# Edge tiles of 124 rows instead of 128 in a three-layer relational graph kernel with gathers from HBM

## The reference

```python
def rgcn_layer(h, W, root, bias):            # W: [8, 256, 256]
    agg = segment_sum(h[src], edge_type * 6250 + dst, 8 * 6250).reshape(8, 6250, 256)
    return einsum('rnd,rde->ne', agg, W) + h @ root + bias
xn = layernorm(x)
h = relu(rgcn_layer(xn, W0, root0, bias0))
h = relu(rgcn_layer(h, W1, root1, bias1))
h = sigmoid(rgcn_layer(h, W2, root2, bias2))
x = x + h + mix(xn)                          # linear attention, 8 heads; MLP 256 -> 1024 -> 256
out = x + moe(layernorm(x))                  # 8 experts, top 2
```

## Time and profile before

| quantity | value |
|---|---|
| time, median of 3 runs | 8040.71 us (8016.86 to 8065.2) |
| profiled execution, span from the first to the last instruction | 6522.0 us |
| profiled execution, its own total time | not given; the span is what the profile tells |
| TensorE matmul, busy | 5410.7 us (83%) |
| TensorE weight load, busy | 4060.0 us (62%) |
| GpSimd, busy | 4625.3 us (71%) |
| VectorE, busy | 2019.4 us (31%) |
| ScalarE, busy | 1061.6 us (16%) |
| moved by DMA | 887.88 MB, mean 136 GB/s |

### The profile page before, as it was taken

The page is one execution under the profiler, slowest core; times in us unless marked ns, Lnnn a source line. Parts: engine busy times, 40 slices in busy tenths (PEclk is TensorE's granted clock), DMA queues, the critical chain, the costliest instruction groups (busy, mean ns, idle before and its releaser), DMA issues.

```text
span 6522.0 us, 82564 instructions
## 1 busy us (share of the span) xinstructions
PE 5410.7 (83%) x22990; PEld 4060.0 (62%) x22990; DVE 2019.4 (31%) x5385; ACT 1061.6 (16%) x2756; POOL 4625.3 (71%) x4909
## 2 busy tenths in 40 slices
PE   8977777777777778888888888887888888888888
PEld 4445555555555546666666666666777777777776
DVE  3321211122222223332333333333444444444444
ACT  2211111111111111111111111111222222222222
POOL 1057777777777767777777777776777777777776
PEclk9989898889898889999999999999999999999999
DMA  6654444444444444544554444444433333433333
GB/s 195 180 155 137 137 137 137 137 137 137 137 137 137 137 143 144 147 146 146 147 148 146 146 145 146 147 146 149 116 115 115 115 115 115 115 115 115 116 115 93
DMA packets 354380, 887.88 MB, mean 136 GB/s; under 512 B 86234, under 2 KB 179294, under 8 KB 335623
## 3 DMA queue, kind: packets, MB, share of 16 engines
q0 software_dynamic: 232080, 633.91, 33.0%
q10 hardware_dynamic: 114178, 243.16, 12.8%
q1 hardware_dynamic: 7740, 5.99, 0.3%
HBM read 697.11 MB, written 185.60 MB: 135 GB/s over the span
## 4 chain that ended last, share of the span: by engine, by line
POOL 44%; PE 30%; issue 15%; ACTq 5%; DMA 3%; ACT 1%; POOLq 1%; DVE 0%; DVEq 0%; SPq 0%
POOL ring L501 44%; PE ps_out L1403 11%; PE ps_y L1371 8%; PE ps_tr L1570 2%; PE ps_b L1558 2%; DMA ring<-table,gather_idx 2%; PE ps_c L1371 1%; PE ps_b L1371 1%; PE ps_c L1558 1%; ACTq L619 1%; ACTq L740 1%; ACTq L699 1%; ACT y_stage L517 1%; PE ps_y L1656 1%; ACTq L527 1%
## 5 line engine op out<-in xcount | busy, mean ns | idle before, releaser
L501 POOL DMA_INDIRECT ring<-table,gather_idx x4836 | 4580.7, 947 | 1519.4 <-issue 1487.8
L1403 PE MATMUL ps_out<-ring,onehot 128*125 x8400 | 2238.3, 419 | 709.7 <-SPq L428 671.1
L1403 PEld LDWEIGHTS ps_out<-ring,onehot 128*125 128x125 f32 x8400 | 1699.0, 209 | 1131.0 <-issue 857.7
L1371 PE MATMUL ps_y<-W,hT 128*125 128x512 f32 (+1 forms) x2400 | 1016.9, 564 | 0.9 <-ACT hT L564 0.9
L835 DVE COPY y_stage<-ps_y 125x512 f32<-125x512 f32 x150 | 103.7, 692 | 2425.6 <-PE ps_y L1371 2393.6
L1403 PE MATMUL ps_out<-ring,onehot_more 128*125 x2448 | 661.3, 421 | 131.9 <-SPq L428 87.4
L1371 PEld LDWEIGHTS ps_y<-W,hT 128*125 128x125 f32 x2400 | 455.8, 192 | 400.1 <-issue 372.7
L994 DVE TENSOR_TENSOR onehot<-targets,ps_out 128x500 f32<-128x500 f32 x1050 | 646.4, 671 | 172.1 <-issue 117.1
L1403 PEld LDWEIGHTS ps_out<-ring,onehot_more 128*125 128x125 f32 x2448 | 479.5, 205 | 286.8 <-issue 214.7
L517 ACT COPY y_stage<-ps_y 125x512 f32<-125x512 f32 x350 | 204.6, 585 | 1659.1 <-PE ps_y L1371 1653.8
L994 DVE TENSOR_TENSOR onehot_more<-targets,ps_out 128x250 f32<-128x250 f32 x612 | 240.9, 414 | 608.4 <-PE ps_out L1403 490.2
(11 more groups left out here) (193 smaller groups left out, 3208.2 us busy)
## 6 DMA issues: line engine op xcount, KB each, us to landing
table<-y_stage ACTq DMA_DIRECT2D x147, 896.0 KB
ring<-table,gather_idx POOLq DMA_INDIRECT x4836, 2.9
table<-y_stage ACTq DMA_DIRECT2D x147, 104.0 KB
xn_in<-xn_scratch ACTq DMA_DIRECT2D x100, 125.0 KB
base<-y_stage ACTq DMA_DIRECT2D x100, 125.0 KB
base_in<-base ACTq DMA_DIRECT2D x100, 125.0 KB
x_in<-in_x_dram ACTq DMA_DIRECT2D x75, 125.0 KB
xn_scratch<-xn_in ACTq DMA_DIRECT2D x50, 125.0 KB
```

Of the source, the lines that this page charges most:

```text
L501: nc.gpsimd.indirect_dma_start(ring[0:n, c * D:(c + 1) * D], None, table[l], bass.IndirectOffsetOnAxis(ap=gather_idx[0:n, tile:tile + 1].b ...
L1371: last = nc.tensor.matmul(BANK[phase][b][0:WIN, 0:n], hT[parity][:, k, :], W[:, k, b * 2 * D:b * 2 * D + n], start=(k == 0), stop=(k == K ...
L1403: return nc.tensor.matmul(ps_out[w % 2][0:WIN, 0:D], lhsT, ring[:, bass.ds(slot + j * D, D)], start=first, stop=last)
```

## The change

TILE becomes 124. A gather moves 124 rows into the first 124 partitions of `ring`, the one-hot matrices have 124 partitions, and the multiplies have 124 rows to add over. The edge lists are loaded with 124 edges to a tile: blocks of 128 tiles remain, with rows of 124 numbers (496 bytes) instead of 128 (512 bytes). RING, TILES and STATIC stay as they are.

206,250 edges now make 1664 tiles (the last with 38 edges) in 416 chunks, all filled, so 4992 gathers in the three layers. Both before and after there are 13 blocks of 128 tiles. In the last, partly filled block there were 75 whole tiles and are 127. From the drawn edge list the units a layer, borders counted twice, come to 465 after, against 452 before.

```diff
--- before.py
+++ after.py
@@ -26,7 +26,7 @@
 
 WIN = 125
 WIN_A = 112
-TILE = 128
+TILE = 124
 TILES = 4
 RING = 8
 STATIC = 7
@@ -92,8 +92,8 @@
         gather_idx = sb("gather_idx", [128, TB * 128], I32)
         targets = sb("targets", [128, TB * 128])
         ring = sb("ring", [128, RING * TILES * D])
-        onehot = [sb(f"onehot{i}", [128, TILES, WIN]) for i in range(STATIC)]
-        onehot_more = [sb(f"onehot_more{i}", [128, HALF, WIN]) for i in range(2)]
+        onehot = [sb(f"onehot{i}", [TILE, TILES, WIN]) for i in range(STATIC)]
+        onehot_more = [sb(f"onehot_more{i}", [TILE, HALF, WIN]) for i in range(2)]
         W = sb("W", [128, K, ROWS * D])
         bias_bc = sb("bias_bc", [WIN, 3, D])
         y_stage = [sb(f"y_stage{i}", [WIN, ROWS * D]) for i in range(2)]
@@ -176,7 +176,7 @@
         bounds_row = qk_all[0:1, :, :].rearrange("p a b -> p (a b)")[:, 0:7 * NB_INTS].rearrange("p (i n) -> p i n", i=7)
 
 
-        PREP = TB * 128
+        PREP = TB * TILE
         prep_i = big[:, 0:PREP].bitcast(I32)
         prep_f = big[:, PREP:2 * PREP]
         prep_d = big[:, 2 * PREP:3 * PREP].bitcast(I32)
@@ -370,7 +370,7 @@
             sp.wait_ge(prep_zeroed, 1)
             for name, dst in (("src", prep_i), ("edge_type_8", prep_t), ("dst", prep_d)):
                 a = t[name]
-                v = dst[:, 0:TB * 128].rearrange("p (b f) -> p b f", f=128)
+                v = dst[:, 0:TB * TILE].rearrange("p (b f) -> p b f", f=TILE)
                 if full_blocks:
                     sp.dma_start(v[:, 0:full_blocks, :], a[0:full_blocks * 128 * TILE]
                                  .rearrange("(b p f) -> p b f", p=128, f=TILE)).then_inc(edges_loaded, 16)
@@ -436,12 +436,12 @@
         @block.gpsimd
         def _(pool):
 
-            lo = full_blocks * 128
-            nc.gpsimd.memset(prep_i[:, lo:TB * 128], 0)
-            nc.gpsimd.memset(prep_t[:, lo:TB * 128], 0)
+            lo = full_blocks * TILE
+            nc.gpsimd.memset(prep_i[:, lo:TB * TILE], 0)
+            nc.gpsimd.memset(prep_t[:, lo:TB * TILE], 0)
 
             nc.gpsimd.memset(order_b[:, ordC - 1:ordC], PADDED)
-            nc.gpsimd.memset(prep_d[:, lo:TB * 128], PADDED).then_inc(prep_zeroed, 1)
+            nc.gpsimd.memset(prep_d[:, lo:TB * TILE], PADDED).then_inc(prep_zeroed, 1)
             nc.gpsimd.memset(ident[:], 1.0).then_inc(consts_made, 1)
             pool.wait_ge(consts_made, 1)
             nc.gpsimd.affine_select(out=ident[:], in_=ident[:], compare_op=ALU.is_equal, fill=0.0,
@@ -496,8 +496,9 @@
                         for j in range(TILES):
                             c = s * TILES + j
                             tile = chunk * TILES + j
-                            n = min(TILE, edges - tile * TILE)
-                            assert n > 0
+                            left = edges - tile * TILE
+                            n = min(TILE, left) if left > 0 else TILE
+                            assert n > 1
                             nc.gpsimd.indirect_dma_start(
                                 ring[0:n, c * D:(c + 1) * D], None, table[l],
                                 bass.IndirectOffsetOnAxis(ap=gather_idx[0:n, tile:tile + 1].bitcast(U32), axis=0)
@@ -881,8 +882,8 @@
 
                 for i in (2 * b, 2 * b + 1):
                     dve.wait_ge(prep_tr, i + 1)
-                    nc.vector.tensor_copy((gather_idx, targets)[i % 2][:, b * 128:(b + 1) * 128],
-                                          ps_out[i % 2][:, 0:128]).then_inc(prep_ev, 1)
+                    nc.vector.tensor_copy((gather_idx, targets)[i % 2][0:TILE, b * 128:(b + 1) * 128],
+                                          ps_out[i % 2][0:TILE, 0:128]).then_inc(prep_ev, 1)
 
             def units_before():
 
@@ -992,8 +993,8 @@
 
             def onehots(out, n, nodes, col, count):
                 return nc.vector.tensor_tensor(
-                    out, targets[:, bass.ds(col, count)].unsqueeze(2).broadcast_to([128, count, n]),
-                    nodes.unsqueeze(1).broadcast_to([128, count, n]), ALU.is_equal)
+                    out, targets[0:TILE, bass.ds(col, count)].unsqueeze(2).broadcast_to([TILE, count, n]),
+                    nodes[0:TILE, :].unsqueeze(1).broadcast_to([TILE, count, n]), ALU.is_equal)
 
             def set_nodes(w):
 
@@ -1310,7 +1311,7 @@
                 else:
                     pe.wait_ge(prep_ev, 2 * b)
                 for src, half in ((prep_f, 0), (prep_df, 1)):
-                    nc.tensor.transpose(ps_out[half][:, 0:128], src[:, b * 128:(b + 1) * 128],
+                    nc.tensor.transpose(ps_out[half][0:TILE, 0:128], src[:, b * TILE:(b + 1) * TILE],
                                         ident[:, :]).then_inc(prep_tr, 1)
 
             def vectors_transposed():
@@ -1401,7 +1402,7 @@
 
             def add_tile(w, lhsT, slot, j, first=False, last=False):
                 return nc.tensor.matmul(ps_out[w % 2][0:WIN, 0:D], lhsT,
-                                        ring[:, bass.ds(slot + j * D, D)], start=first, stop=last)
+                                        ring[0:TILE, bass.ds(slot + j * D, D)], start=first, stop=last)
 
             def unit(l, w, i):
```

## The result

The changed kernel takes 8462.96 us (median of 4 runs, 8461.52 to 8464.06), the kernel before 8035.37 us (4 runs, 8016.86 to 8065.2). The ratio is 1.053, 95% interval 1.0506 to 1.0553: 427.6 us slower, where 215 us were forecast. The sign was right and the size was not; 8463 us lies above the range.

What follows compares the result with a forecast made beforehand. GpSimd's gather beat was taken as the bound. 156 more gathers added 184 us (8225) or 234 us (8275), all other terms 0; the middle, 8250 us (+2.6%), was forecast, range 8170 to 8340 us.

Steps and rivals of the forecast that it cites:

- the data of the gathers: Indirect queue's transfers: row numbers 16 does not divide still go over all 16 engines, far from the limit; cost 0.
- the gathers: GpSimd's gather line, main term: 156 more gathers at a beat of 1.248 us, +184 us.
- over 4 engines: Rival, gather transfers: 4 us more if the four engines change; 10,881 us if always the same four, chance 0.03.
- The sum's basis: Whole run: +184 us if 1518.7 us outside the span stand apart, +234 if gathers carry them; middle 8250 us.
- upper end: Whole run: 1518.7 us spread over the gathers, beat 1.564 us, 156 more gathers less 10 us for rows: 8275 us.
- what bounds the kernel now: GpSimd's gather line: engine full at a steady 1.25 us beat, gathers 6056 of 6522 us.
- Count of gathers: GpSimd's gather line: 4836 gathers become 4992, adding 184 to 234 us.
- Edge lists: Phase 0 loads: 0 to 27 us more, covered by 30.7 us before VectorE needs them; taken as 0.
- TensorE and VectorE at 0: Multiplies and one-hot work: 39 more units, 22.5 us a layer on TensorE, hidden under waits and gathers; cost 0.
- Rows are what is paid: Rival, GpSimd's gather time goes with rows moved, so nothing changes: 8041 us, within 0.5%; chance 0.07.
- faster: Rival, GpSimd's beat: 124-row gathers much cheaper than 128, below 1.211 us; -41 us, 8000 us; chance 0.05.
- layer 2 held by TensorE: Rival, layer 2 windows: up to 22.5 us, with late edge lists 27 more, 8300 us; above 8340 us 0.03.

Runs made afterwards that it cites:

- second profile of before: The kernel before, unchanged, profiled again: 8009.5 us [8034.8], with the profile covering the run this time.
- the pauses: Kernel before with one or three small memsets on GpSimd behind each gather: one column 7816.3 us, three 7868.3 [8016.2]; 192 columns lagging 7772.3, 96 lagging 8001.0 [7888.0].

## Why the prediction was wrong in size

**The step that failed** is "the data of the gathers". It read 4833 x 48 + 3 x 32 = 232,080 packets as proof that 42 rows go over all 16 engines, and so 124 too. The same numbers come out with 14 engines and two idle ones that get a placeholder packet each: 16 + 16 = 32. The argument against 14 (30 packets) took for granted that an idle engine has none. A count that two readings share had been taken for evidence of one. The rule of the Trainium skill, "DMA: Bandwidth & Descriptors", section "Why a DMA increments its semaphore by 16 and not by 1", that a DMA goes over the largest number up to 16 that divides its rows, holds for these gathers, and the trace agrees at every row count tried (718,704 packets at 124 rows). Its own exception for some direct copies by GpSimd plays no part here.

**With it fell the price** of a 124-row gather in "the gathers". The slope of 0.0005 us a row between 42 and 128 rows was 3 rows an engine against 8: 0.043 us for five, 0.009 each. 124 rows stand at 31 on that scale, not beside 128. (Carried on, this slope would give 1.14 us; it steepens beyond 8.) Forecast 0.944 us, measured 1.292; forecast beat 1.248, measured 1.596 to 1.599.

**The rival "over 4 engines"** had the spread right and its price wrong. It priced the transfer, 4 us if the engines change, and nothing for GpSimd. The sign that it named for 4 engines, a later landing, was there: SyncE's wait for a chunk ended 4.8 us after the start of the chunk's last gather at the median, against 2.8 in both profiles of before. That the engines do change is to be read off the kernel with 127 rows: one engine has a gather's data, by the shares of the earlier trace rows some 7 us of engine time, and the gathers start 2.89 us apart. On one and the same engine 4884 of them would take some 34,000 us (an estimate), and the run took 14,562.

**The sum's basis** was right in its upper end and wrong in its picture. The step "what bounds the kernel now" read a steady GpSimd beat of 1.25 us, which is true of the execution shown (6522 us) and not of those timed (about 8035 us): there a gather advances every 1.564 us, the value that the forecast's upper end had worked out from the 1518.7 us. Here it is measured (7561.7 / 4835). That the two agree is no proof of its picture, a gather that is slower when nobody looks: both spread the same run time over the same gathers. What fills the 0.31 us is not the gather, whose length is 0.949 us, but stalls for late hand-offs.

That is also why a gather 0.34 us longer cost so little. Against the kernel with 4992 gathers of 128 rows, GpSimd's busy time on them grew from 4737.0 to 6455.9 us, +1719, and its idle time before them fell from 3054.6 to 1564.6 us, -1490. First gather to last is 229 us longer, and the tail 26 us shorter; the spans differ by 205 us, the medians by 194. Had the stalls been nothing, as in the profile of before, the same length would have cost nearly 1719 us.

**The terms one by one.** Count of gathers: forecast +184 to +234, the middle taken as 8250 us (+215 against the 8035 measured), measured +234 together with the next term, so that this term was sized well although its upper end rested on a wrong picture; that part is luck. Edge lists: 0 was taken with a bound of 27; VectorE starts on them 17.0 us later and the first gather 17.6. In the changed kernel this is SyncE's issue of the single row behind the last partly filled block, and VectorE's first use, the counterpart of the earlier trace rows. SyncE's timeline:

```profile
14.78 4.98 SPq L380 DMA_DIRECT2D big<-in_src_dram  x1
24.43 12.05 SPq L380 DMA_DIRECT2D big<-in_edge_type_dram  x1
42.42 10.14 SPq L380 DMA_DIRECT2D big<-in_dst_dram  x1
```

VectorE's timeline:

```profile
76.75 1.84 DVE L869 SCALAR_TENSOR_TENSOR big<-big 128x1612 f32<-128x1612 int32 x1 [32.15 <-DMA ring<-in_dst_dram]
```

The load issued behind the 127 rows (L380, the last, unfilled tile) took 4.98, 12.05 and 10.14 us to issue, where it took 0.25 to 0.29 us in the second profile of before. L387 was then issued at 54.20 instead of 28.79, VectorE started at 76.75 instead of 59.77, and the first gather at 406.7 instead of 389.1. Idle time before this instruction was named as the sign of a wrong step, and it was there. The last block has 127 rows with tiles of 124 alone, and 127 has no divisor up to 16 but 1; the kernels with 126, 127 and 112 have 100, 88 and 49 rows in that block, and their gathers start at 386 to 388 us. That the 127 is the reason is read off this, no run changed it alone. TensorE and VectorE at 0: right, L1404 has 8400 + 2760 = 11,160 instructions as forecast, all under waits for landings. "Rows are what is paid" fell with 64 against 62 rows, "faster" with the 1.292 us, "layer 2 held by TensorE" with a wait for chunks of 620 us there instead of 5.5.

**Left open**: what limits ordinary executions to about 1.56 us a gather when gathers are short. This mean is nearly the same with 112, 126 and 128 rows (1.559, 1.567, 1.561), which differ in bytes per gather and in TensorE's work, is 1.51 to 1.57 with the pauses that leave a beat of 1.25 to 1.39, and 1.63 with 64 rows. It is no fixed price of a gather: the three layers of the second profile of before advance by 1.49, 1.54 and 1.63 us. The trace shows semaphores that move late and names no cause. Nor is it known why the execution first profiled had none, or why a memset of one column takes away 2.5%.

## What to carry to other kernels

Before the row count of an indirect gather is changed, find its largest divisor up to 16: with rows of 1 KB the rows per engine set the time that GpSimd spends on it, so 124 rows cost more than 128, and 127 nearly three times as much. Compare the profile's span with the timed runs first: if it is a fifth shorter, its bound may not be theirs, and the profile has to be taken again before anything is priced. A packet count proves a way of spreading only when the other ways have been counted with everything that they could send.

## What the runs showed of the hardware that was not expected

An engine that gets no row of a gather still gets packets of 4-byte entries, as many as a used one has data packets (144 packets for 4 x 31 rows, 528 for 1 x 127). A gather of 38 rows (1.11 us) is longer than one of 128 (0.949 us). A semaphore that TensorE raises moved 11.5 us after the multiply had ended, and more than 1 us late for 325 of 700 such multiplies in an 8008 us execution; in another execution of the same kernel, of 6522 us, for none. GpSimd waited 1563 us for places in the first and 31.6 us in the second.
